# Six loads of 48, 32 and 16 rows for the query and key stack, in place of twelve of 16

## The reference

```python
q = einsum('bnsd,neod->bneso', sx, wq)      # 4 heads n, 4 experts e, width 16
k = einsum('bnsd,nod->bnso', sx, wk)
v = einsum('bnsd,nod->bnso', sx, wv)
scores = einsum('bnesd,bntd->bnest', q, k) * d ** 0.5 + causal
att = softmax(scores); qkv = einsum('bnest,bntd->bnesd', att, v)
# then: experts mixed by a gate, residual, layer norm, a two-layer net, layer norm, output gate
```

## Time and profile before

| | us |
|---|---|
| median of three runs | 3402.48 |
| the three runs | 3365.5, 3402.48, 3409.38 |
| profiled execution, time | 3390.36 |
| profiled execution, span | 3388.6 |
| mean granted clock of TensorE | 0.92 of full speed |

### The profile page before, as it was taken

How to read it: one execution, slowest core, us unless ns; L and a number is a source line. 1 busy time by engine, 2 the same in 40 slices (tenths; PEclk the granted TensorE clock), 3 DMA queues, 4 the chain that set the end, 5 groups by cost and what they waited for, 6 DMA issues and landing times.

```text
span 3388.6 us, 81043 instructions
## 1 busy us (share of the span) xinstructions
PE 3081.6 (91%) x24964; PEld 2193.7 (65%) x24964; DVE 2615.6 (77%) x7699; ACT 1817.5 (54%) x4484; POOL 1301.8 (38%) x1368
## 2 busy tenths in 40 slices
PE   0699999999999899998999998999999999999995
PEld 0588888888888634444777776666666666666663
DVE  4788888888888578886888865788777777778773
ACT  0355555555555445554766643555555555555552
POOL 1443444434344144441000022445445444444432
PEclk9999999999999989997888867999889989989996
DMA  4100000000000000000000013443333333333420
GB/s 140 35 22 22 14 21 14 21 20 15 21 14 8 1 1 0 0 0 1 1 0 0 0 28 58 71 66 64 59 59 59 58 59 60 70 57 63 68 36 4
DMA packets 74280, 110.98 MB, mean 33 GB/s; under 512 B 20105, under 2 KB 65481, under 8 KB 73577
## 3 DMA queue, kind: packets, MB, share of 16 engines
q1 hardware_dynamic: 72936, 106.85, 16.9%
q10 hardware_dynamic: 1024, 0.39, 0.0%
HBM read 76.01 MB, written 30.82 MB: 32 GB/s over the span
## 4 chain that ended last, share of the span: by engine, by line
PE 25%; issue 9%; POOL 6%; DMA 6%; DVE 5%; SPq 2%; ACT 1%; POOLq 0%; DVEq 0%; ACTq 0%
DMA qe_K<-query_key_parts 4%; PE psum L2329 3%; PE psum L1660 3%; PE psum L2315 2%; PE psum L2343 2%; POOL qe_root L3032 2%; PE psum L2302 2%; DMA query_key_parts<-qe_parts 2%; PE psum L2366 2%; PE psum L1689 2%; PE psum L1677 1%; SPq L2221 1%; PE psum L1731 1%; SPq L2223 1%; POOL qe_parts L3014 1%
## 5 line engine op out<-in xcount | busy, mean ns | idle before, releaser
L2782 DVE TENSOR_REDUCE qe_top<-psum 125x1 f32<-125x375 f32 (+2 forms) x896 | 500.8, 596 | 238.1 <-PE psum L2302 235.7
L2589 ACT ACTIVATE qe_E<-psum 125x375 f32<-125x375 f32 (+1 forms) x896 | 459.0, 531 | 285.1 <-PE psum L2302 261.0
L2302 PE MATMUL psum<-bconst 125*125 125x125 bf16 (+2 forms) x1792 | 491.3, 274 | 0.0
L625 PE MATMUL psum<-Q,K 96*125 96x125 f32 (+3 forms) x2304 | 404.5, 311 | 0.5 <-ACT E L836 0.4
L2315 PE MATMUL psum<-qe_K,qe_Q 96*125 96x375 bf16 (+2 forms) x1536 | 332.0, 300 | 59.4 <-DMA qe_K<-query_key_parts 32.3
L625 PEld LDWEIGHTS psum<-Q,K 96*125 96x125 f32 (+1 forms) x2304 | 334.3, 189 | 24.5 <-issue 1.2
L2329 PE MATMUL psum<-qe_Q,qe_K 97*125 97x375 bf16 (+2 forms) x1536 | 336.8, 299 | 2.4 <-ACT qe_E L2589 2.0
L1175 POOL TENSOR_TENSOR Q<-rot 64x375 f32<-64x375 f32 (+1 forms) x256 | 305.7, 1213 | 73.4 <-DVE rot L976 61.4
L836 ACT ACTIVATE E<-psum 125x500 f32<-125x500 f32 x384 | 226.2, 589 | 172.7 <-PE psum L645 169.5
L2315 PEld LDWEIGHTS psum<-qe_K,qe_Q 96*125 96x125 bf16 x1536 | 182.4, 148 | 167.1 <-DVE qe_top L2782 71.6
L2302 PEld LDWEIGHTS psum<-bconst 125*125 125x125 bf16 x1792 | 266.4, 149 | 9.8 <-issue 6.9
(11 more groups left out here) (341 smaller groups left out, 7199.7 us busy)
## 6 DMA issues: line engine op xcount, KB each, us to landing
qe_Q<-query_key_parts SPq DMA_DIRECT2D x192, 187.5 KB, 6.2
query_key_parts<-qe_parts SPq DMA_DIRECT2D x32, 843.8 KB, 3.6
s_row<-scores SPq DMA_DIRECT2D x32, 366.2 KB
qe_K<-query_key_parts SPq DMA_DIRECT2D x192, 46.9 KB, 6.6
x_tokens<-x SPq DMA_DIRECT2D x32, 187.5 KB
x_chunks<-x SPq DMA_DIRECT2D x4, 750.0 KB
E<-x SPq DMA_DIRECT2D x4, 750.0 KB
out<-qe_hout SPq DMA_DIRECT2D x32, 93.8 KB
```

The costliest lines, as they stand in the source:

```text
L625: nc.tensor.matmul(out[:, first * TP:(first + n) * TP].rearrange("p (o q) -> p o q", o=n), t.K[0:rows(h), par, h, jt * TP:(jt + 1) * TP], ...
L2302: return nc.tensor.matmul(out, B("ident_b")[0:TP, 0:TP], rhs, start=False, stop=True, skip_group_check=True)
L2589: nc.scalar.activation(E[:, e % 2, a:a + width], bank[0:TP, 4 + n % 2, 0:width], ACT.Exp).then_inc(e_done, 1)
L2782: nc.vector.tensor_reduce(dst, src, AX, ALU.max).then_inc(m_read, 1)
```

## The change

The columns of the query and key weights are reordered, so that a projected tile's row r is (d, head, expert) rather than (head, expert, d), and a part's 16 rows of width d lie one behind the other in DRAM. The DRAM tensor is flat: first the three parts of the queries, then those of the keys, each part as 128 rows. The store becomes two DMAs, queries (384 pieces of 1500 bytes) and keys (384 pieces of 750 bytes), with a semaphore each; ScalarE waits for both.

The six groups are put in another order: key part 0 with query parts 0, 1 and 2; key part 1 with query parts 0 and 1; key part 2 with query part 0. They are the same six products. For key part 0 one DMA loads 48 rows of queries (parts 0 to 2 lie one behind the other in DRAM), another loads the 16 key rows three times, into 48 rows of K. For key part 1 it is 32 rows each, for key part 2 it is 16. A row of Q now comes as one piece of 12,000 bytes, one of K as one piece of 3000 bytes.

```diff
@@ weight_layout
-    heads = z(D, 4, HE, 2, DH2)
+    queries, keys, values = z(D, 2, DH2, HE, 2), z(D, 1, DH2, 2, HE), z(D, 1, HE, 2, DH2)
     for n in range(HE):
         rows = slice(n * DH2, (n + 1) * DH2)
         for e in range(EE):
-            heads[rows, e % 2, n, e // 2] = l["wq"][n, e].T
-        heads[rows, 2, n, 0] = l["wk"][n].T
-        heads[rows, 3, n, 0] = l["wv"][n].T
-    k.add("w_heads", heads.reshape(D, 4, 128))
+            queries[rows, e % 2, :, n, e // 2] = l["wq"][n, e].T
+        keys[rows, 0, :, 0, n] = l["wk"][n].T
+        values[rows, 0, n, 0] = l["wv"][n].T
+    k.add("w_heads", np.concatenate([v.reshape(D, -1, 128) for v in (queries, keys, values)], 1))
@@ query_experts
-    q_parts, k_parts = (0, 0, 1, 0, 1, 2), (0, 1, 0, 2, 1, 0)
-    RS = len(q_parts) * DH2
+    RUNS = (3, 2, 1)
+    RS = sum(RUNS) * DH2
@@ sync
-            rows_of = qk_dram.rearrange("(a d) p i s -> p d a i s", d=DH2)
-            keys_of = qk_dram.rearrange("(h a d) p i s -> a p i d h s", a=2, d=DH2)
+            NQ = NP * 128 * 2 * S
+            queries = qk_dram[0:NQ].rearrange("(p r s) -> p r s", p=NP, r=128)
+            keys = qk_dram[NQ:].rearrange("(p r s) -> p r s", p=NP, r=128)
+            query_rows = queries.rearrange("p (d a) s -> (p d) (a s)", d=DH2)
+            key_rows = keys.rearrange("p (d h) s -> p d (h s)", d=DH2)
 
             def stack(b, slot):
 
                 wait(sp, e_ready, (b - 2) * NU)
-                wait(sp, stacked, b * 32 * len(q_parts))
+                wait(sp, stacked, b * 32 * len(RUNS))
                 sp.wait_ge(parts_done, (b + 1) * NP)
-                sp.dma_start(qk_dram, parts[:]).then_inc(parts_stored, 16)
+                sp.dma_start(queries.rearrange("p r s -> r p s"), parts[:, :, 0:2, :].rearrange("r p i s -> r p (i s)")
+                             ).then_inc(parts_stored, 16)
+                sp.dma_start(keys.rearrange("p r s -> r p s"), parts[:, :, 2, :]).then_inc(keys_stored, 16)
                 sp.wait_ge(parts_stored, (b + 1) * 16)
-                for g, (qp, kp) in enumerate(zip(q_parts, k_parts)):
-                    rows = slice(g * DH2, (g + 1) * DH2)
-                    sp.dma_start(Q[rows, slot].rearrange("d (a i) s -> d a i s", i=2), rows_of[qp, :, :, 0:2]
-                                 ).then_inc(stacked, 16)
-                    sp.dma_start(K[rows, slot], keys_of[0, kp, 2]).then_inc(stacked, 16)
+                sp.wait_ge(keys_stored, (b + 1) * 16)
+                at = 0
+                for kp, n in enumerate(RUNS):
+                    rows = slice(at, at + n * DH2)
+                    sp.dma_start(Q[rows, slot].rearrange("d q s -> d (q s)"), query_rows[0:n * DH2]).then_inc(stacked, 16)
+                    sp.dma_start(K[rows, slot].rearrange("d h s -> d (h s)"),
+                                 key_rows[kp:kp + 1, :, 0:HE * S].to_broadcast((n, DH2, HE * S))).then_inc(stacked, 16)
+                    at += n * DH2
@@ scores_for_max
-                    pe.wait_ge(stacked, (b + 1) * 32 * len(q_parts))
+                    pe.wait_ge(stacked, (b + 1) * 32 * len(RUNS))
@@ first_part
                 if i == 0:
                     wait(act, parts_stored, b * 16)
+                    wait(act, keys_stored, b * 16)
@@ kernel
-    qk_dram = nc.dram_tensor("query_key_parts", (128, 3, 3, S), BF16).ap()
+    qk_dram = nc.dram_tensor("query_key_parts", (128 * 3 * 3 * S,), BF16).ap()
```

More of the change, by code:

```diff
@@ L2178, in query_experts @@
         folded, set_up, p_ready, v_ready, nz_ready, nz_done, v_kept = map(sem, ("folded", "set_up", "p", "v", "nz", "nz_done", "v_kept"))
-        hi_done, full_done, parts_done, parts_stored, stacked = map(sem, ("hi", "full", "parts", "parts_stored", "stacked"))
+        hi_done, full_done, parts_done, parts_stored, keys_stored, stacked = map(
+            sem, ("hi", "full", "parts", "parts_stored", "keys_stored", "stacked"))
         m_ready, m_read, neg_ready, neg_turned, maxT_kept = map(sem, ("m", "m_read", "neg", "neg_turned", "maxT"))
```

## The result

| | median us | runs | ratio to before (95%) |
|---|---|---|---|
| before | 3392.2 | 4, 3365.5 to 3409.4 | |
| changed | 3474.7 | 4, 3455.7 to 3479.1 | 1.024 (1.016 to 1.032) |

The kernel before has a fourth run here, hence 3392.2 in place of 3402.5.

What follows compares the result with a forecast made beforehand. TensorE was taken to bound the stage, not always at full clock. Savings of 49+9+11+15+3 us, less 5 for ScalarE, made 82 us: median 3402.5-82 = 3320 us, range 3285 to 3400.

Steps and rivals of the forecast that it cites:

- The threshold: At the gate of a TensorE step: if L falls under 17.5 us, no step waits for the stack.
- L: Latency from a step's store to the last landing of its loads: 18.2 us before, 14.8 us forecast.
- The sum: Whole kernel: 82 us saved if L falls under 17.5 us, median 3402.5 to 3320 us.
- The full-speed step of 35.5 us: Steady part: a TensorE step without its DMA wait takes 35.5 us, from 35.8 less its own wait of 0.6.
- The five us I put down for ScalarE: ScalarE's first_part waits for the longer store, in front of exponentials TensorE needs: +5 us in all.
- The store: One store DMA becomes two: +0.5 us on L, between bounds of +0.3 and +4 us.
- The loads: Twelve stack loads become six wider ones: 10.5 us instead of 14.4, worst case 14.4.
- 1 us for the repeated key rows: Part of the 10.5 us for the stack's loads: the copied key rows add 1 us.
- the mechanism as a rival: Key loads: copies outermost confine the DMA to three and two engines; at 7.5 GB/s an engine, +310 us; chance 0.12.
- halfway: Middle case of the copied key loads: 12 GB/s an engine, L 20.6 us, step 43.1 us, +65 us, 3467 us.
- The clock: TensorE steps after a DMA wait start at 1.2 GHz, about 6 us slower matmuls; without waits this goes.
- Fewer issues, layout, weights: SP issues fall from 6.2 to about 2.8 us a step, weights' columns and DRAM layout permuted: 0 us.

Runs made afterwards that it cites:

- the first rows of the table: Three kernels against the changed one: rows ordered width first; each key copy its own load; width first plus first query load before the keys' landing: 3314, 3314, 3308 us.
- width first: Changed kernel with the stack's rows ordered (d, copy) instead of (copy, d), queries and keys alike, store still in two: 3313.9 us, ratio 0.980.
- the run with small pieces: Against the changed kernel with each key copy its own load: one store of 384 pieces of 2250 B, loads in 1500 and 750 B pieces: 3325.8 us, ratio 0.985.

## Why the prediction was wrong, point by point

**The threshold: right.** TensorE stands at the gate 17.65 us after the store in the changed kernel too (median), and the three kernels with L under it in nearly every step (the first rows of the table) have no wait to speak of.

**The sum, if L falls under it: right.** I had 82 us for it, 3308 from the profiled execution or 3320 from the median. The kernels that get there have 3308 to 3314, 67 to 74 us under before. The full-speed step of 35.5 us should have been 35.2 by its own working (35.8 less 0.6), which makes 4 us over the twelve steps that use it. The five us I put down for ScalarE don't show: its waits for the stores rose from 5.9 us in 7 places to 31.7 in 30 (width first), but TensorE waits for E 2.0 us in 7 places in both.

**The store: mis-sized.** I took +0.5 us "since the 128-row side stays", from a range of 0.3 to 4. It was 5.2 against 3.8 us at the first load, +1.4, and +1.4 in the median too (5.05 against 3.62). Smaller pieces may be a part of it: the one store of 384 pieces landed in 4.0, and the pair has 768. Alone the split took L from 18.0 to 19.3 and the time up by 100 us. I had priced its effect on ScalarE and on L, but set it only against a gain in L that I took for certain; the present L was 0.5 us over the threshold already, so even my half microsecond would likely have cost something, which no run shows.

**The loads: the failing step.** "10.5 us" became 14.0. The part of the term on wide loads was near: with the keys spread over all engines the six loads took 11.5 us, where 10.5 less the 1 us for the copies is 9.5, at 152 GB/s and not the 218 taken for the wide pairs. What failed is "1 us for the repeated key rows": they cost about 2.5 us (14.0 against 11.5), and that keeps L at 19.0 instead of 16.7, with the same store. I had the mechanism as a rival, and priced an engine that carries both copies at 8.6+2 us if it runs at 20 GB/s, "which is in my term". It runs at 21 GB/s at the end, but over all the loads a busy engine moved 12.4 GB/s. The likely course of it is argued, since the trace names no engines: while all sixteen work, the loaded ones get no more than the others; the key rows of the first load stand before the later query rows in the same engine's order; and only when the rest is idle do they run faster. What the windows show is 14 engines at work for 7.3 us and 3.5 for another 6.6. At the 12 GB/s that I called halfway, I had L = 20.6 and 3467; it was 19.0 and 3475. That the times are so near is luck in part: that L is 1.6 us too long, and each microsecond of L over the threshold cost more than I had reckoned, since it makes steps slow. A bound halfway to a rival is a price, and deserved more than 0.12 in all.

The Trainium skill says this in "DMA: Bandwidth & Descriptors", "Rules for kernel authors": a leading zero-stride broadcast of c copies holds the DMA to at most c engines. With the share of 0.13, 2.1 engines, at the end of the two-copy load, and 161 us for moving that dimension inward, the runs agree. I gave the page's rule the time of its own engine and not that of the queue it makes. For the wide loads, "SBUF — State Buffer", section "Door 1: The DMA port swizzle", in the Trainium skill gives some 218 GB/s for partitions 0 to 63, over eight ports; measured were 152, with the 16-row loads and the out store among them.

**The clock.** That a wait costs the slower matmuls behind it was right and carried the sum. I used it only downwards. It goes both ways: the kernel before lay at the edge, with 8 of its 20 gates away from the loop's turn followed by a slow step. 1 us more in L made it 18 of 20 (changed). The length of the wait doesn't settle it: waits of 0.71 and 1.05 us before were followed by a step at 1.00, waits of 0.74 and 1.25 us by one at 0.87 and 0.84. In the changed kernel two equal waits, with the windows of their steps:

```profile
2241.80 0.37 PE L2324 MATMUL psum<-qe_K,qe_Q 96*125 96x375 bf16 x1 [1.22 <-DMA qe_K<-query_key_parts]
...
2355.91 0.57 PE L2324 MATMUL psum<-qe_K,qe_Q 96*125 96x375 bf16 x1 [1.22 <-DMA qe_K<-query_key_parts]
...
2241.80:2278.30 36.50, 34.47 (x312) 23.67 (x312) 31.66 (x75) 22.26 (x51) 19.52 (x23) 1.00 0.30 67
2355.90:2401.10 45.20, 40.81 (x312) 27.49 (x312) 31.95 (x75) 22.55 (x51) 19.37 (x23) 0.84 0.24 56
```

In width first and in the run with small pieces one step is slow (0.87 and 0.88) with no DMA wait before it and away from the turn. What else decides is open.

**Fewer issues, layout, weights: not contradicted.** No run has them alone; the fast kernels have the layout and the weights' columns too, and come out near the sum that counts them as nothing.

**Still open:** why the second store, a third of the bytes, lands so much later than the single one did. The moving of the bytes is the smaller part. Windows of the end of a store, until the first load goes out, in the changed kernel and in the one before:

```profile
2732.00:2733.60 1.60, 1.60 (x12) 0.46 (x11) 1.39 (x8) 0.69 (x2) 0.00 (x0) 1.00 0.05 10
...
2681.20:2681.90 0.70, 0.70 (x7) 0.60 (x7) 0.64 (x4) 0.25 (x2) 0.00 (x0) 1.00 0.12 23
```

From 3.5 us after the first issue on, the pair has next to nothing under way, and still lands at 5.1; the single store is at that point after 3.1 us and lands at 3.8. So the packets end some 0.5 us later and the landing follows them by some 0.9 us more. What fills that time isn't shown, and no run separates a second DMA from the number and size of the pieces, or changes the order of the two.

## What to carry to other kernels

A load chain that ends just at the moment its user arrives is not hidden; price both signs of a change to it, and from the edge on, with what the clock does behind each wait. Before a load is widened by a copied source, look at which dimension is outermost: with two or three copies there, about two engines were left at work at the end, and with the 16 rows there the same loads were 2.5 us faster. If two transfers must both land before the next begin, let the next ones that need only the first go ahead.

## What the runs showed of the hardware

- A DMA whose source has three or two copies outermost ends with about two engines at work, 44 GB/s in all; with the 16 rows outermost the same six loads take 11.5 instead of 14.0 us.
- Loads into 48, 32 and 16 rows reach 152 GB/s where loads into 16 rows each reach 109; pieces of 12,000 and 3000 B instead of 1500 and 750 are worth 0.9 us of a stack's loads (11.6 against 12.5), and the kernel has 3314 against 3326 us, with the store's difference in it.
- A store of 844 KB lands in 3.6 us as 128 pieces, in 4.0 as 384, and as two DMAs with 768 pieces, the second issued 0.4 to 0.6 us behind, in about 5; 0.9 us of that lie behind the last packets.
- 1.7 us of latency in a place with about a microsecond of slack behind it cost 57 us over 27 steps and 91 us in the median of the kernel; 37.3 instead of 22.1 us of waiting went with 53 us more of busy time on TensorE, at a mean clock of 0.87 instead of 0.92.
